# Feed-forward and key/value products of a four-layer cross-attention kernel: plain fp32 operands in place of a three-product high/low split

## The reference

```python
kh = (kv_in @ wk + bk).reshape(b, t, H, K)
vh = (kv_in @ wv + bv).reshape(b, t, H, K)
...
h = jax.nn.gelu(h @ w_fc1 + b_fc1, approximate=False) @ w_fc2 + b_fc2
```

## Time and profile before

| | us |
|---|---|
| median of 3 runs | 919.29 |
| lowest, highest | 918.73, 924.12 |
| span of the profiled execution | 921.3 |
| PE busy in it | 830.0 |
| DVE busy | 549.2 |
| ACT busy | 407.6 |
| POOL busy | 364.8 |
| mean granted TensorE clock | 0.967 |

### The profile page before, as it was taken

How to read it: one execution, slowest core, us unless ns; L and a number is a source line. 1 busy time by engine, 2 the same in 40 slices (tenths; PEclk the granted TensorE clock), 3 DMA queues, 4 the chain that set the end, 5 groups by cost and what they waited for, 6 DMA issues and landing times.

```text
span 921.3 us, 13090 instructions
## 1 busy us (share of the span) xinstructions
PE 830.0 (90%) x4823; PEld 615.4 (67%) x4823; DVE 549.2 (60%) x1090; ACT 407.6 (44%) x965; POOL 364.8 (40%) x384
## 2 busy tenths in 40 slices
PE   3899999999399799689999999999999879877798
PEld 3788888877289355466665676666566668734588
DVE  3665757664944599655545665333279666559744
ACT  1676676856232377634432232444223232148331
POOL 3474544545600488651203662000076542247400
PEclk9999999999799999999999999999999989889799
DMA  6300000000000500002422000212100000200001
GB/s 180 124 2 1 1 1 1 1 1 2 0 1 7 177 1 1 1 1 92 137 92 92 1 1 1 82 58 101 37 0 1 1 1 1 91 1 1 1 12 35
DMA packets 24004, 30.87 MB, mean 34 GB/s; under 512 B 3628, under 2 KB 16773, under 8 KB 23941
## 3 DMA queue, kind: packets, MB, share of 16 engines
q1 hardware_dynamic: 23400, 30.03, 10.0%
q10 hardware_dynamic: 540, 0.01, 0.0%
HBM read 28.98 MB, written 1.05 MB: 33 GB/s over the span
## 4 chain that ended last, share of the span: by engine, by line
PE 70%; DVE 13%; issue 6%; POOL 5%; ACT 4%; ACTq 1%; DMA 1%; POOLq 0%; DVEq 0%
PE wide_ps L436 8%; PE narrow_ps L455 7%; PE narrow_ps L607 7%; PE wide_ps L741 7%; PE wide_ps L755 6%; PE wide_ps L483 6%; PE wide_ps L707 5%; PE narrow_ps L790 5%; PE wide_ps L728 3%; DVE scoresb L1227 2%; DVE mx L1236 2%; PE wide_ps L416 2%; PE wide_ps L709 2%; POOL probs L1519 2%; DVE sums L1243 2%
## 5 line engine op out<-in xcount | busy, mean ns | idle before, releaser
L912 ACT ACTIVATE probsT<-wide_ps 128x640 f32<-128x640 f32 (+1 forms) x104 | 86.0, 827 | 137.9 <-PE wide_ps L483 137.0
L1511 POOL TENSOR_TENSOR scoresb<-scoresb,mx 128x768 f32<-128x768 f32 (+1 forms) x40 | 70.7, 1767 | 191.3 <-DVE mx L1234 151.1
L1531 POOL TENSOR_TENSOR probs<-scoresb,rcp 128x512 f32<-128x512 f32 (+1 forms) x128 | 91.3, 735 | 78.1 <-DVE rcp L1311 78.1
L483 PE MATMUL wide_ps<-ident,probs 128*128 128x128 f32 x640 | 90.6, 280 | 29.1 <-POOL probs L1519 23.7
L483 PEld LDWEIGHTS wide_ps<-ident,probs 128*128 128x128 f32 x640 | 73.1, 143 | 56.5 <-issue 54.9
L1497 POOL TENSOR_TENSOR rstd<-veps,mhalf 128x1 f32<-128x1 f32 x56 | 32.0, 572 | 159.5 <-DVE veps L1162 159.5
L607 PE MATMUL narrow_ps<-probsT,vpad 128*64 128x128 f32 x640 | 83.4, 278 | 1.4 <-ACT xq L912 1.4
L1519 POOL TENSOR_TENSOR probs<-scoresb,rcp 128x1024 f32<-128x1024 f32 x40 | 78.8, 1971 | 7.8 <-DVE rcp L1244 7.8
L607 PEld LDWEIGHTS narrow_ps<-probsT,vpad 128*64 128x64 f32 x640 | 68.2, 137 | 13.8 <-issue 11.1
L436 PE MATMUL wide_ps<-xq_r,wstream_r 128*128 128x512 f32 x192 | 64.4, 419 | 8.5 <-issue 6.8
L912 ACT ACTIVATE headbuf<-wide_ps,col 128x256 f32<-128x256 f32 x68 | 28.5, 470 | 96.2 <-PE wide_ps L711 85.4
(11 more groups left out here) (161 smaller groups left out, 1644.3 us busy)
## 6 DMA issues: line engine op xcount, KB each, us to landing
wstream<-in_L_xattn_wq SPq DMA_DIRECT2D x8, 512.0 KB, 4.1
wstream<-in_L_xattn_wk SPq DMA_DIRECT2D x8, 512.0 KB, 5.0
wstream<-in_L_xattn_wv SPq DMA_DIRECT2D x8, 512.0 KB, 6.1
wstream<-in_L_xattn_wo SPq DMA_DIRECT2D x8, 512.0 KB, 7.6
wstream<-in_L_xattn_mlp_w SPq DMA_DIRECT2D x2, 1024.0 KB, 6.0
wstream<-in_L_xattn_w_fc SPq DMA_DIRECT2D x2, 1024.0 KB, 6.8
xq<-in_x SPq DMA_DIRECT2D x1, 1024.0 KB, 5.8
wstream<-in_L_xattn_fc_w SPq DMA_DIRECT2D x1, 1024.0 KB, 5.1
```

The lines of the kernel that those rows point to most:

```text
L483: m = nc.tensor.transpose(ps[:, j * P:(j + 1) * P], probs[:, u % 2, j * P:(j + 1) * P], ident[:])
L912: nc.scalar.activation(dst, src, ACT.Identity, **kw).then_inc(ring.drained[ring.slot(key)], 1)
L1511: g.tensor_tensor(s3[:, first:], s3[:, first:], mx[:, u % 3, first:].unsqueeze(2).broadcast_to([P, 16 - first, n_scores]), ALU.subtract).t ...
L1531: g.tensor_tensor(probs[:, u % 2, o:o + 2 * n].rearrange("p (i k) -> p i k", i=2), s3[:, :, lo:hi], rcp[:, u % 3, 0:2].unsqueeze(2).broadc ...
```

## The change

All splits go. The feed-forward lines and line 707 multiply the loaded weights with `actT`, the hidden activations and `ctxT` as plain fp32, one product in place of three. ACT writes GELU's result straight to `hidden`, which now lies in `region` (it is free during all three feed-forward layers). `mlp` on DVE keeps only the residual additions. The up groups wait for ACT's drain of the transposes, down waits for GELU's drain, both for the weights' DMA. Layer 3's feed-forward weights get a place of their own in `wstream`, and their load waits for the last value product of layer 2's second head loop (`VW`, 1, 7) and not for the end of layer 2's feed-forward layer.

```diff
-                            for i, (pw, px) in enumerate(PARTS):
-                                if fp == 0 and j == 0 and kc == 0 and px == 1:
-                                    pe.wait_ge(x_split, 2 * (2 * n + half) + 2)
-                                m = mm(ps[:, j * 512:(j + 1) * 512], w1[pw][:, kc, f * P:(f + 1) * P],
-                                       xparts[px][:, kc, half * 512:(half + 1) * 512],
-                                       start=kc == 0 and i == 0, stop=kc == NC - 1 and i == 2)
+                            m = mm(ps[:, j * 512:(j + 1) * 512], w1[:, kc, f * P:(f + 1) * P],
+                                   actT[:, kc, half * 512:(half + 1) * 512], start=kc == 0, stop=kc == NC - 1)
...
-                                    pe.wait_ge(hidden_split, 8 * n + 4 * (q // 4) + f // 2 + 1)
-                                for part, (pw, ph) in enumerate(PARTS):
-                                    m = mm(ps[:, 0:D], hidden[:, ph, f, qoff((q + i) % 4)], w2[pw][:, f, :],
-                                           start=f == 0 and part == 0, stop=f == NF - 1 and part == 2)
+                                    pe.wait_ge(*wide.empty(("up", n, q // 4, f // 2)))
+                                m = mm(ps[:, 0:D], hidden[:, q // 4, f, qoff((q + i) % 4)], w2[:, f, :],
+                                       start=f == 0, stop=f == NF - 1)
...
-                for m in range(2):
+                for m, w in enumerate((wk, wv)):
                     for kc in range(NC):
-                        for i, (w, part) in enumerate(((high, 0), (low, 0), (high, 1))):
-                            mm(ps[:, m * 256:(m + 1) * 256], w[:, m, kc, :], cparts[:, part, kc, :],
-                               start=kc == 0 and i == 0, stop=kc == NC - 1 and i == 2)
+                        mm(ps[:, m * 256:(m + 1) * 256], w[:, kc, o:o + P], ctxT[:, kc, :],
+                           start=kc == 0, stop=kc == NC - 1)
...
-            sp.wait_ge(*narrow.full(("down", 1, NQ - 1)))
-            sp.dma_start(*halves(mlp_load(2, 0), t["L3_xattn_fc_w"])).then_inc(load["mlp3"], 16)
-            sp.dma_start(*halves(mlp_load(2, 1), t["L3_xattn_proj_w"])).then_inc(load["mlp3"], 16)
+            sp.wait_ge(*wide.full(("VW", 1, 7)))
+            sp.dma_start(*halves(mlp_weights(2, 0), t["L3_xattn_fc_w"])).then_inc(load["mlp2"], 16)
+            sp.dma_start(*halves(mlp_weights(2, 1), t["L3_xattn_proj_w"])).then_inc(load["mlp2"], 16)
...
-                            nc.scalar.activation(scoresb[:, i % 3, j * 512:(j + 1) * 512],
+                            nc.scalar.activation(hidden[:, half, f, :],
...
-                    v.tensor_copy(xparts[0][:, :, cols], actT[:, :, cols]).then_inc(x_split, 1)
-                    dve.wait_ge(x_split, 2 * (2 * n + half) + 1)
-                    v.tensor_tensor(xparts[1][:, :, cols], actT[:, :, cols], xparts[0][:, :, cols].bitcast(F32), ALU.subtract
-                                    ).then_inc(x_split, 1)
...
-                if step in (22, 38):
-                    weights_low(0, step // 38)
...
-                if h + 2 < H2:
-                    kv_low(a, h + 2)
...
-                if 5 <= step < 7:
-                    weights_low(2, step - 5)
```

More of the change, by code:

```diff
@@ L182, in build @@
         region = sb("region", [P, 16416])
+        hidden = region[:, 0:8192].rearrange("p (h f n) -> p h f n", h=2, f=NF)
         w0 = wstream
@@ L188, in build, with mlp_weights @@
         out_w0 = w0[:, 1536:2048].rearrange("p (c n) -> p c n", c=NC)
[L190 to L211, removed]
+        MLP_AT = (2048, 0, 4096)
+        def mlp_weights(n, which):
+            at = MLP_AT[n] + 2048 * which
+            return wstream[:, at:at + 2048].rearrange("p (c n) -> p c n", c=(NC, NF)[which])
         q_w1 = wsmall[:, 0:512].rearrange("p (c n) -> p c n", c=NC)
@@ L937, in mlp @@
             def mlp(n, func, b1):
-                act.wait_ge(prob_ready, probcount[base["1"] if n == 0 else base["3"] if n == 1 else len(probcount) - 1])
                 for half in range(2):
@@ L1038, in _ @@
                     exp0(step + 2)
-                if step in (20, 36):
-                    act.wait_ge(load["mlp0"], 32)
-                    mlp_high(nc.scalar.copy, 0, step // 36).then_inc(w_high, 1)
             act.wait_ge(*wide.full("cols"))
@@ L1046, in _ @@
             norm_turned(0, "L0_postnorm_w", None)
-            act.wait_ge(*narrow.full(("proj", 0, NQ - 1)))
-            for chunk in (2, 3):
-                mlp_high(nc.scalar.copy, 0, chunk).then_inc(w_high, 1)
             mlp(0, ACT.Gelu_apprx_tanh, "L0_mlp_b1")
@@ L1109, in attend2 @@
                         exp(u0 + step + 2, 16 * 65)
-                    if a == 1 and 2 <= step < 6:
-                        if step == 2:
-                            act.wait_ge(load["mlp2"], 32)
-                            act.wait_ge(*wide.full(("VW", 1, 7)))
-                        mlp_high(nc.scalar.copy, 1, step - 2).then_inc(w_high, 1)
             precompute2(0)
@@ L1135, in _ @@
                     exp(base["3"] + step + 2, 1024)
-                if 4 <= step < 8:
-                    act.wait_ge(load["mlp3"], 32)
-                    mlp_high(nc.scalar.copy, 2, step - 4).then_inc(w_high, 1)
             norm_turned(6, "L3_ln2_w", "L3_ln2_b")
@@ L1191, in add_residual, with mlp @@
                                 ).then_inc(narrow.drained[narrow.slot(key)], 1)
[L1193 to L1219 removed]
+            def mlp(residual):
+                for q in range(NQ):
+                    residual(q)
             def front(u, n, scale, addend, n_scores, bias=None):
@@ L1332, in _ @@
             dve.wait_ge(*wide.empty("cols"))
-            mlp(0, 0, lambda q: add_residual(("down", 0, q), xA, q, 1))
-            def kv_low(a, h):
-                dve.wait_ge(kv_high, a * H2 + h + 1)
-                loaded, high, low = kv_weights(a, h)
-                for m in range(2):
-                    ins = v.tensor_tensor(low[:, m], loaded[:, m], high[:, m].bitcast(F32), ALU.subtract)
-                ins.then_inc(kv_split, 1)
-            def split_operands(a):
-                dve.wait_ge(prob_ready, probcount[base["2a" if a == 0 else "2b"]])
-                link(v.tensor_copy(cparts[:, 0], ctxT[:]))
-                v.tensor_tensor(cparts[:, 1], ctxT[:], cparts[:, 0].bitcast(F32), ALU.subtract).then_inc(ctx_split, 1)
-                for h in range(2):
-                    kv_low(a, h)
+            mlp(lambda q: add_residual(("down", 0, q), xA, q, 1))
             def spread_bias_values(a):
@@ L1376, in _ @@
                           mask1[:, q, :].unsqueeze(1).broadcast_to([P, 16, T]), T)
-                if step == n1 + 1:
-                    split_operands(0)
                 q = done1(step)
@@ L1458, in _ @@
                                   ).then_inc(wide.drained[wide.slot(("v", 3))], 1)
-            mlp(1, 4, lambda q: stream_norm(5, q, q - 1 if q else None, ("down", 1, q), xB, 5))
+            mlp(lambda q: stream_norm(5, q, q - 1 if q else None, ("down", 1, q), xB, 5))
             norm(5, NQ - 1)
```

98 lines of the change are left out of this document (15 added, 83 removed).

## The result

The changed kernel takes 935.4 us (median of 4 runs, 934.4 to 936.7); the kernel before, on the same chip, 921.3 us (4 runs, 918.7 to 924.1). The ratio is 1.014, 95% interval 1.012 to 1.017: slower by 1.4%. The forecast was 932.5 us, with 925 to 939 as its range. So a difference of a few us between two single profiles can be scatter.

A forecast was written before the change was run, and what follows sets the result against it. PE was taken to bound the kernel, with 70% of the chain. Growth of 37.4 us less gains of 24.2 gave +13.2, added to the median of 919.3: 932.5 us, 1.4% slower, range 925 to 939.

The forecast's parts named there:

- Feed-forward growth, +29.6: Three feed-forward layers: plain products add 5.0 us up and 4.9 down a layer, +29.6 us in all.
- Head growth, +0.26 a round: Key/value group in layer 2's head loops: 1.61 us becomes 1.87, over 30 rounds +7.8 us; bounds +0.12 and +0.31.
- Start of layer 0's feed-forward, -6.8: PE's 6.8 us stand for DVE's input copy beside POOL goes; line 1168's wait and 2.5 us of half clock stay.
- Start of layer 2's, -6.6: Second feed-forward layer starts after DVE's last value copy, not line 1204's beside POOL: gain 6.6 us, no half clock counted.
- Start of layer 3's, -0.4: Third feed-forward layer starts when its transposes end, with 2.6 us of half clock kept: gain 0.4 us.
- Self-attention, 0; second attention, -2.7: Removed weight splits gain nothing in self-attention, 2.7 us in the second cross attention of the 16-head layer.
- Layer 3's attention, -4.8: Last attention: two DVE subtractions and the norms behind them go, 5.2 us, taken as 4.8; bounds 2.4 and 6.
- Starts of the loops, -2.9: Second head of each head loop comes 1.3 and 0.35 us earlier, with 1.2 less half clock: gain 2.9, bounds 1 and 4.5.
- the clock case: Rival: half clock goes with the stalls at two feed-forward starts and the head loops; 926.2 us, chance 0.18.
- The dear case: Rival: heads' key/value group at 1.92 us and only one hold gained in the last attention; 936.4 us, chance 0.12.
- The POOL case: Rival: DVE's relief also removes 14 us of PE's waits for POOL's probabilities; 918.5 us, not slower, chance 0.07.
- The case 4:3: Rival: each plain product in feed-forward and heads lasts as long as four split ones; 954.5 us, chance 0.03.

The follow-up runs named there:

- e1: Changed kernel with line 707's three-product split form and the key/value splits put back; 927.0 us, ratio 1.005 to the kernel before.
- e5: Changed kernel with the old weight-split instructions back at their old steps, writing spare memory nobody reads; 941.4 us, ratio 1.021 to the kernel before.
- e6: Changed kernel with the value-bias product's 16 stationary columns padded to 128; 925.9 us, ratio 1.004 to the kernel before.
- e3: Changed kernel with POOL's key spreading for layer 1 held until all norms of the layer before are out; 927.0 us, ratio 1.004.
- e4: Kernel before, POOL's key spreading held until layer 0's hidden activations (for layer 1) or layer 2's feed-forward input (for layer 3) are split; 903.5 us, 0.979.
- e8: e7 with line 741's 64 stationary columns also padded to 128 in every even head; 892.0 us, ratio 0.966 to the kernel before.
- e7: e4 with the value-bias product's 16 stationary columns padded to 128; 898.9 us, ratio 0.976 to the kernel before.
- e2: Kernel before with only line 707 plain and the head splits gone; 928.5 us, ratio 1.006 to the kernel before.

## Why the prediction was right, point by point

The total came out at +11.5 us of span where +13.2 was forecast, and 935.4 us where 932.5 was; 1.9 us lie between span and time in the profiled run. The forecast stood on a median of 919.3, which one more run moved to 921.3; on that base it would have been 934.5. It is right in sign, mechanism and size, but partly because misses of both signs cancel: the growth came out 1.2 us larger and the gains 3.1 larger than in the sum.

- **Feed-forward growth, +29.6.** Right. From first to last down record +6.6 us in layers 0 and 3, with 40 records of 0.429 in place of 60 of 0.234 ahead of them, +3.1: 9.7 a layer, 29.2 in all.
- **Head growth, +0.26 a round.** The reasoning that failed, though the size is small. It took line 741's 1.87 as the likeness of the new group. But that group holds the cost of its own changes of column number, 1.87 - 1.73 = 0.14, and the split group already held 1.61 - 1.42 = 0.19 of its own, which stays. The growth is the bare difference, 8 x 0.216 - 12 x 0.118 = 0.31, the upper bound, and so +9.3 and not +7.8.
- **Start of layer 0's feed-forward, -6.8.** The stand went as said (7.23 to 0.21), and line 1077 kept its 7.14. Of the 2.5 us of half clock, kept in the sum, only 18.31 - 17.2 = 1.1 was paid in this profile. (The 2.5 went up to a record's modelled end, 266.39; from start to start it is 16.39 - 14.1 = 2.3.) It is not a gain of the change: e1, e5 and e6 have the same 40 records behind the same stand of 6.78 us, and they took 19.7, 18.6 and 19.8 us, at granted clocks of 0.87, 0.92 and 0.87, against 18.35 and 0.94 in the changed kernel and 17.24 at full clock in e3. So 1.1 to 2.5 us are paid here by the same code. Measured: 9.7 - (2.0 + 6.6) + 7.0 = 8.1.
- **Start of layer 2's, -6.6.** Measured 9.7 - (5.9 - 2.5) + 0.7 = 7.0. The first record follows the last value copy (line 1316) by 0.09 us, at full clock, as assumed; the chain of the changed kernel there, and at layer 3's start:

```profile
748.61 0.31 DVE region L1316
748.92 0.09 issue
749.01 17.41 PE wide_ps L384 x40
...
873.01 0.44 PE wide_ps L356 x2
873.45 18.87 PE wide_ps L384 x40
```

- **Start of layer 3's, -0.4.** Measured 9.7 - 8.6 = 1.1; again less half clock than before (18.87 for 40 records, so 1.7 instead of 2.6). This, too, scatters: 19.3 to 19.9 in e1, e3, e5 and e6.
- **Self-attention, 0; second attention, -2.7.** Right; e5 shows both.
- **Layer 3's attention, -4.8.** Measured -4.8, and 5.1 with the same instructions put back in e5. Its bounds (one hold, 2.4; both and no closing, 6) held. This size is less sharp than it looks: with the same code the attention took 61.8 to 64.9 us over e1, e3, e6 and the changed kernel, at granted clocks of 0.93 to 0.89.
- **Starts of the loops, -2.9.** Measured: head 1 0.5 and 0.2 earlier where 1.3 and 0.35 were said; but its rounds took 6.00 in both loops, growth included, where 7.03 and 7.21 stood, so 1.3 + 1.5 us of half clock went where 1.2 was counted. Together -3.5. The total is right in part by luck: the norms gave little (0.7 where 1.65 was said), the clock much.
- **DMA, 0.** Right: the load that is issued 130 us earlier shows in no stage.

The sum by measurement: +29.2 + 9.4 - (8.1 + 7.0 + 1.1 + 2.7 + 4.9 + 3.5) = +11.3, and +0.3 from the small stages.

Of the rivals, the clock case came true in part: 1.4 + 0.9 + 1.6 us more than my sum. The first two are what scatters between profiles of the same code; the 1.6 at the loops' starts is steadier, since all five kernels with plain heads ran head 1 at full clock in both loops. The dear case was right on the heads and wrong on the last attention. The POOL case did not occur: layer 1, where those waits lie, changed by 0.1 us. The case 4:3 is out with the pitches: a plain product of 512 columns costs 0.858 us, 1.22 times the three split ones and not 4/3 of them.

What I had not seen at all is the question that e3 and e4 answer: the gains in the sum were read as gains of the change, though the two largest were named in the prediction with their true cause, POOL's spreading, beside them.

## What to carry to other kernels

Price a multiplication by the pitch of its records in the chain, per product of operands: three fp32r products take 18% less than one plain fp32 product here, at 512 and at 256 moving columns, as long as the splitting is off the path. When a change gains by removing an instruction that was held up by another engine, try to move what holds it up before you count the gain for the change: 10 of the 21.7 us between the two forms were such stalls, and one added wait at each of two places removed them. In a loop that is gapless on TensorE, look for groups whose stationary operands have another number of columns than their neighbours'; padding to the same number gave 0.25 us for each removed pair of changes with 16 columns and 0.34 for one with 64, and took the ratio from 0.979 (e4) to 0.966 (e8), in which some 3 of 14.3 us of span are full clock at the loops' starts.

## What the runs showed of the hardware that I had not expected

- **The change of stationary columns.** The last record before each change starts its successor 0.093 us late, and the first one after it lasts longer by 0.052 (128 to 64 columns), 0.104 (64 to 128), 0.010 (128 to 16) or 0.058 (16 to 128): 0.10 to 0.20 us a change, for plain and split products alike. That it goes with the number of columns is shown by e6 to e8, in which padding alone removed it. Padding also makes the product write 128 output partitions, so the two are not told apart; nor is it shown why the record is late.
- **The same stand, another clock.** TensorE's windows over head 1 of the loops (columns as in the earlier trace rows). In the kernel before, where it had stood 2.05 and 1.56 us, the granted clock is near 0.77:

```profile
398.10:405.10 7.00, 7.00 (x30) 5.00 (x30) 3.65 (x7) 1.81 (x5) 6.61 (x10) 0.78 0.00 0
567.70:574.90 7.20, 7.20 (x31) 4.77 (x31) 2.87 (x7) 1.81 (x5) 0.00 (x0) 0.76 0.01 2
```

In the changed kernel, after stands of 1.29 and 1.06 us, it is full:

```profile
399.30:405.30 6.00, 6.00 (x27) 3.79 (x27) 1.44 (x3) 1.30 (x4) 5.69 (x9) 1.00 0.00 0
...
572.10:578.10 6.00, 6.00 (x27) 3.79 (x27) 1.44 (x3) 1.30 (x4) 0.00 (x0) 1.00 0.00 0
```

In e7, after stands of 2.31 and 1.82 us, it is 0.76 twice:

```profile
383.80:390.80 7.00, 7.00 (x30) 5.46 (x30) 3.67 (x7) 1.81 (x5) 6.61 (x10) 0.76 0.00 0
549.80:557.00 7.20, 7.14 (x31) 5.32 (x31) 2.87 (x8) 1.81 (x5) 0.00 (x0) 0.76 0.01 2
```

In e8, after stands of 2.31 and 1.81 us, with the same instructions between the attention before and the stand, it is full:

```profile
384.70:389.80 5.10, 5.07 (x31) 4.63 (x31) 3.33 (x6) 1.81 (x5) 4.79 (x8) 1.00 0.00 0
546.80:551.90 5.10, 5.08 (x31) 4.63 (x31) 2.56 (x7) 1.81 (x5) 0.00 (x0) 1.00 0.01 3
```

The other kernels fit the first three: e1 and e4 with stands of 2.06 and 2.07 us and then 1.56 and 1.57 have 0.77 and 0.76; e2, e3 and e5 with 1.26 and 1.06 to 1.07, and e6 with 1.52 and 1.32, have 1.00. So in nine of the ten profiled kernels the shorter stands go with the full clock, and e8 shows that the length of the last stand does not by itself decide whether the clock falls to its lower level. What else does stays open, and one profile of each kernel can't tell it. A round of a head in part at half clock costs 1.3 to 1.7 us more, and where it comes was what the sum could forecast least.
